# A decoder layer for four sequences on one core: PSUM banks in a ring, the causal mask on GpSimd, maxima as a stream, fill matmuls

## The chip, the cores and the metric

One core of a Trainium2 chip runs the kernel. The metric is device time in microseconds (us) of one execution, the median of several. Engines are named as in the profile: PE is TensorE (matmuls; PEld its weight loads), DVE is VectorE, ACT is ScalarE, POOL is GpSimd, SP issues DMAs. PSUM is the memory that PE writes its results to; it has eight banks of 512 fp32 columns.

## The reference

`x` is (4, 512, 512): four sequences of 512 tokens. For each, three residual blocks on layer-normalised input:

```python
x = x + attn(layernorm(x))      # 16 query heads of 32, one shared key and value head, causal
x = x + xattn(layernorm(x), fside, ctx)   # two SmoothQuant int8 linears with silu(gate) * up between
x = x + ffn(layernorm(x))       # gated, 1376 hidden, with shared LoRA and 8 rank-8 experts, top 2
```

The part that the change touches is the attention:

```python
scores = einsum('bqhd,bkd->bhqk', q, k) * scale
scores = where(tril, scores, finfo.min)
attn = softmax(scores, axis=-1)
ctx = einsum('bhqk,bkd->bqhd', attn, v)
```

## The kernel before

**Numbers.** Products that must keep fp32 accuracy are split in a high and a low part (fp32r) and made of three matmuls (`three`, L934 to L937). For the scores the three parts are stacked along the contraction: `qst` and `kst` have 96 rows, and two more rows carry the negated row maximum.

**Attention of one sequence (batch b).** Heads are worked on in four groups `g` of four. First the row maxima: `max` steps compute scores with queries on partitions (L1011), add the causal mask, DVE reduces each row (`negm`, L1295); a `rows` step transposes the 16 x 128 maxima (L1018) and SP moves them by DMA into `qst`. Then 16 steps (g, kt), kt from 3 down to 0: `scores` computes the scores again transposed, keys of tile kt on partitions and n = 512 - 128 kt queries along the columns (L1031); ACT takes the exponential into `probs` (L811); `values` multiplies them with v and with ones into `av` and `den` (L1045). `sums` and `context` normalise (DVE L1310, L1315, L1318), `split_context` makes the high (ACT) and low part (POOL L707), `out` is the output projection. The values of a step are placed behind the scores of the next, and `probs` holds two steps.

**Masks.** Both kinds of scores get their causal mask from PE: before the scores, matmuls of the identity with a mask tile in bf16 write -1e38 or 0 into PSUM with start=True (L1007 for the maxima, L1029 for the transposed scores), and the scores are added on them.

**PSUM.** `slots` are two places of two banks each, handed out in turn (`Tenants`) to every step of attention and of the middle block; `av` and `den` have a bank each; `ring` is two single banks for weight preparation and feed-forward. Whoever claims a place waits until the tenant before it has been read. A `max` unit has 2 or 4 heads spread over both banks of its slot (6 units for each group of heads, `MAX_GROUPS`), a `scores` step is two pairs of heads, one head in each bank.

**Order.** Steps come from four streams: A (attention), L (middle block: a serial chain with DVE, ACT and POOL), F (feed-forward, nearly all matmuls) and W (weights split once and stored). Hand-made strings of letters (`FIRST`, `SECOND`, `STEADY`, `LAST`) say which stream gives the next step; every engine runs its part of all steps in this one order. The `max` steps are part of A, at places that `MAX_AMONG` and `MAX_BEFORE` set. Attention of b = 0 runs with W beside it, then attention of b = 1 with the middle block of b = 0, and from the first `gate` step on F runs beside both.

## Time and profile before

| | us |
|---|---|
| median of 3 runs (1016.59 to 1024.69) | 1017.0 |
| the profiled execution | 1015.68 |
| its span, first to last instruction | 1013.9 |
| PE busy | 923.5 |
| DVE busy | 616.7 |
| ACT busy | 313.1 |
| POOL busy | 248.5 |

Busy is the union of an engine's instructions. A matmul's time in the trace includes its way through the array, so consecutive matmuls overlap in it: what one costs PE is read from start to start. The granted clock is 1.00 at 2.4 GHz and one half at 1.2 GHz; a mean over a stretch lies between. "<-" in a row of waits names what the engine waited for.

### The profile page before, as it was taken

What the parts mean: (1) busy time and instruction counts of PE and PEld (TensorE: products, weight loads), DVE (VectorE), ACT (ScalarE), POOL (GpSimd) and SP (SyncE); (2) the same over time, 40 slices, a digit from 0 to 9 for tenths busy, and PEclk for the clock granted to TensorE, in tenths of its full rate; (3) what the DMA queues carried; (4) which work ended last, traced back from release to release, by engine and by line L of the source; (5) the groups of instructions that cost most, each with busy time, mean ns of one, the idle gap of its engine ahead of it and who ended that gap; (6) DMA issues with size and microseconds to landing.
All of it is one profiled execution on the core that took longest, in us unless ns stands there. A gap on an engine that the chain in (4) does not pass through costs nothing.

```text
span 1013.9 us, 13146 instructions
## 1 busy us (share of the span) xinstructions
PE 923.5 (91%) x5206; PEld 654.6 (65%) x5214; DVE 616.7 (61%) x865; ACT 313.1 (31%) x496; POOL 248.5 (25%) x217
## 2 busy tenths in 40 slices
PE   2898899587999999999999999999979999779997
PEld 1664456454457776667577776666757787568785
DVE  2345768778687687767565886765477565332222
ACT  2323442244353215342423135333222431121110
POOL 3612322421543022123210131231204033011110
PEclk9857979688799999999999999999999999999999
DMA  8963651832666843348344733354335455525442
GB/s 277 312 189 116 233 216 24 246 128 88 238 197 253 202 172 123 126 171 340 116 154 93 230 123 104 147 226 141 107 140 199 152 185 209 205 94 206 161 170 89
DMA packets 42913, 174.98 MB, mean 173 GB/s; under 512 B 5404, under 2 KB 8220, under 8 KB 32868
## 3 DMA queue, kind: packets, MB, share of 16 engines
q1 hardware_dynamic: 36804, 119.09, 34.7%
q10 hardware_dynamic: 6048, 55.05, 14.9%
q8 instruction: 42, 0.69, 0.3%
q14 instruction: 19, 0.16, 0.0%
HBM read 127.52 MB, written 33.75 MB: 159 GB/s over the span
## 4 chain that ended last, share of the span: by engine, by line
PE 74%; DVE 13%; issue 4%; DMA 3%; SPq 3%; ACT 2%; POOL 1%; POOLq 0%; DVEq 0%; ACTq 0%
PE ring L935 12%; PE ring L937 11%; PE ring L936 11%; PE av L1045 4%; PE slot L1031 4%; DVE negm L1295 4%; PE ring L1177 3%; PE den L1045 3%; PE slot L1011 3%; SPq L573 3%; PE slot L935 3%; PE slot L936 2%; PE slot L937 2%; PE slot L1114 2%; PE slot L1029 2%
## 5 line engine op out<-in xcount | busy, mean ns | idle before, releaser
L734 POOL TENSOR_TENSOR hd_l<-hd,hd_h 128x512 fp32r<-128x512 f32 x44 | 57.7, 1312 | 401.2 <-ACT hd_h L909 401.2
L935 PE MATMUL ring<-xT_h,gu 128*128 128x512 f32 x352 | 145.6, 414 | 5.0 <-DVE gated L1502 2.9
L936 PE MATMUL ring<-xT_l,gu 128*128 128x512 f32 x352 | 138.4, 393 | 0.0
L937 PE MATMUL ring<-xT_h,gu 128*128 128x512 f32 x352 | 138.3, 393 | 0.0
L1295 DVE TENSOR_REDUCE negm<-slot 128x4 f32<-128x512 f32 (+2 forms) x96 | 98.6, 1043 | 59.6 <-PE slot L1011 59.0
L811 ACT ACTIVATE probs<-slot 128x256 f32<-128x256 f32 (+3 forms) x128 | 85.0, 700 | 89.8 <-PE slot L1031 89.8
L935 PEld LDWEIGHTS ring<-xT_h,gu 128*128 128x128 f32 x352 | 66.8, 190 | 29.4 <-issue 11.5
L937 PEld LDWEIGHTS ring<-xT_h,gu 128*128 128x128 f32 x352 | 66.6, 189 | 14.9
L1541 DVE TENSOR_TENSOR total<-ring,total 128x512 f32<-128x512 f32 x64 | 44.0, 688 | 51.0 <-PE ring L937 50.9
L1031 PE MATMUL slot<-qst,kst 98*128 98x128 f32 (+3 forms) x256 | 74.8, 387 | 0.0
L936 PEld LDWEIGHTS ring<-xT_l,gu 128*128 128x128 f32 x352 | 67.0, 190 | 11.6
L1011 PE MATMUL slot<-kst,qst 96*128 96x128 f32 (+3 forms) x256 | 73.4, 397 | 0.0
L935 PE MATMUL ring<-dn,hd_h 128*128 128x512 f32 x176 | 70.1, 398 | 0.2 <-DVE ad_sum L1521 0.2
L937 PE MATMUL ring<-dn,hd_l 128*128 128x512 f32 x176 | 69.2, 393 | 0.0
L936 PE MATMUL ring<-dn,hd_h 128*128 128x512 f32 x176 | 69.1, 393 | 0.0
L909 ACT ACTIVATE hd_h<-hd 128x512 fp32r<-128x512 f32 x44 | 27.8, 631 | 119.1 <-DVE hd L1513 119.1
L905 ACT ACTIVATE gated<-ring 128x512 f32<-128x512 f32 x44 | 26.3, 599 | 122.5 <-PE ring L1177 122.3
L1513 DVE SCALAR_TENSOR_TENSOR hd<-gated,ring 128x512 f32<-128x512 f32 x44 | 30.2, 687 | 51.7 <-PE ring L1177 36.1
L1502 DVE SCALAR_TENSOR_TENSOR gated<-gated,ring 128x512 f32<-128x512 f32 x44 | 29.9, 680 | 50.5 <-ACT gated L905 50.5
L1315 DVE RECIPROCAL rden<-rden 128x256 f32<-128x256 f32 x32 | 55.8, 1744 | 0.1
L1029 PE MATMUL slot<-mask_bf 128*128 128x128 bf16 x256 | 38.8, 236 | 16.9 <-DVE negm L1295 7.7
L1045 PE MATMUL av<-probs,v 128*32 128x512 f32 (+3 forms) x512 | 52.3, 484 | 1.3 <-DVE cx L1310 1.1
(194 smaller groups left out, 1754.2 us busy)
## 6 DMA issues: line engine op xcount, KB each, us to landing
gu<-gu_parts ACTq DMA_DIRECT2D x42, 1280.0 KB, 5.5
dn<-dn_parts SPq DMA_DIRECT2D x12, 1728.0 KB, 7.7
gu_parts<-gu SPq DMA_DIRECT2D x11, 1280.0 KB, 5.7
qst<-qT_h SPq DMA_DIRECT2D x64, 128.0 KB, 2.4
raw_gu<-gu SPq DMA_DIRECT2D x11, 640.0 KB, 7.3
dn_parts<-dn SPq DMA_DIRECT2D x11, 576.0 KB, 7.7
dn<-dn_parts SPq DMA_DIRECT2D x4, 1152.0 KB, 5.1
x_in<-x SPq DMA_DIRECT2D x8, 512.0 KB, 4.8
```

Source lines behind the costliest of these rows:

```text
L734: pool.tensor_tensor(hd_l[:, i, :], hd[:, i, :], hd_h[:, i, :].bitcast(F32), ALU.subtract).then_inc(hd_lo.sem, 1)
L811: act.activation(probs[:, 2 * (step % 2) + pr, :, 0:n], slots[SLOT["scores", b, step, pr]][:, :, 0:n], ACT.Exp, scale=SCALE).then_inc(p_re ...
L935: pe.matmul(out_, w_hi_, m_hi_, start=start, stop=False, skip_group_check=True)
L936: pe.matmul(out_, w_hi_, m_lo_, start=False, stop=False, skip_group_check=True)
L937: return pe.matmul(out_, w_lo_, m_hi_, start=False, stop=stop, skip_group_check=True)
L1011: mm = pe.matmul(ps[:, bank, at * n:(at + 1) * n], qst[0:KROWS, 4 * g + h0 + h, qt * P:(qt + 1) * P], kst[0:KROWS, 0:n], start=False, stop ...
L1029: pe.matmul(ps[:, j, 0:P], mask_bf[:, 0, :], mask_bf[:, 2, :], start=True, stop=False, skip_group_check=True)
L1031: mm = pe.matmul(ps[:, j, 0:n], kst[0:KROWS + 2, kt * P:(kt + 1) * P], qst[0:KROWS + 2, 4 * g + 2 * pr + j, kt * P:T], start=False, stop=T ...
L1045: mm = pe.matmul(to[HD * c:HD * c + HD, kt * P:T], weights, probs[:, 2 * (step % 2) + c // 2, c % 2, 0:n], start=(kt == TT - 1), stop=(kt ...
L1295: dve.tensor_reduce(negm[:, h0:h0 + heads, qt].rearrange("p (a c) -> p a c", a=2), slots[SLOT["max", b, g, i]][:, :, 0:heads // 2 * n].rea ...
L1315: dve.reciprocal(rden[:, cols], rden[:, cols]).then_inc(rden_ready.sem, 1)
L1541: dve.tensor_tensor(total[:, tt, :], ring[RING["down", b, s, tt]][:, :], total[:, tt, :], ALU.add)\
```

## The change

Five edits in one.

1. **Banks.** The four banks of the two slots become one ring of single banks. `Banks.claim` hands out one, or two neighbouring ones for the tenants in `BANK_WIDTH`; two at the end of the ring start again at bank 0. It waits for the release of each bank taken. A `q` step takes a bank of its own where two shared a slot.
2. **Units of one bank.** `MAX_GROUPS` is 11 units for each group of heads (4 heads of 128 columns; 2 of 256, twice; 1 of 384 and 1 of 512, four times each), `SCORES` splits each step in the same way: 1, 2, 4 and 4 units for kt = 3, 2, 1, 0. So there are 176 units of each kind for 96 `max` units and 128 pairs.
3. **The transposed scores' mask** is no longer added by PE (L1029 goes, 256 matmuls). ACT's exponential signals `p_exp`, and POOL then sets the upper part of the diagonal 128 x 128 block of each head in `probs` to 0 with an affine select; `values` wait for POOL. The bank is free as soon as ACT has read it.
4. **Maxima** are a stream X of their own, and one string `TURNS` gives the whole order, anew.
5. **Fills.** A digit n in `TURNS` is n matmuls of the bf16 identity with 256 columns of `mask_bf` into the ring bank that is next in turn, after its last reader and without claiming it. There are 428 of them in 154 places; 94 stand before the first transposes, 226 between the first `max` unit and the first `gate` step, 89 behind that. PE waits for the masks at its start.

```diff
+class Banks:
+    def claim(self, eng, key, signal, value):
+        first, width = bank_after(self.next, BANK_WIDTH.get(key[0], 1))
+        assert self.table[key] == (first, width), key
+        for bank in range(first, first + width):
+            if bank in self.left and (bank == first or self.left[bank] != self.left[first]):
+                eng.wait_ge(*self.left[bank])
+        for bank in range(first, first + width):
+            self.left[bank] = (signal.sem, value)
+        self.next = first + width
+        return self.banks[:, first:first + width, :]
...
-MAX_GROUPS = ((0, 0, 4), (1, 0, 4), (2, 0, 2), (2, 2, 2), (3, 0, 2), (3, 2, 2))
+    def upcoming(self, eng):
+
+        place = self.n % 2
+        if place in self.left:
+            eng.wait_ge(*self.left[place])
+        return self.places[place]
...
+BANKS = 4
+BANK_WIDTH = {"turn1": 2, "out": 2, "turn": 2, "s_rows_ps": 2, "turn_a": 2, "turn_w": 2, "product0": 2, "product1": 2}
+MAX_GROUPS = [(qt, h, min(4, TT // (qt + 1))) for qt in range(TT) for h in range(0, 4, min(4, TT // (qt + 1)))]
...
+SCORES = [[(h, min(4, TT // (TT - kt))) for h in range(0, 4, min(4, TT // (TT - kt)))] for g, kt in STEPS]
...
+def bank_after(bank, width):
+    return (0 if bank + width > BANKS else bank), width
+
+
+def maxima_steps(b):
+
+    for g in range(4):
+        for i in range(MG):
+            yield ("max", b, g, i)
...
-    "AAAAAAAAAAAAAAWAWWAAWAAAWAAAAAWWAAAAAAAAAAAAAAAAAAAAAAAAAAAWAWWAAAAAWAAWAAAAAAWAAAAWAAAAAAAAAAAAAAAAAAAAAAAAAA"
...
+TURNS = (
+    "A1A111114111111111114111111414111AA4444111111111111194111141AA1114A14AAAAA1AAA1W41WWAAWAX14XX11X1114X1XXX41XXW"
...
+            def scores(b, step, unit):
+                h0, heads = SCORES[step][unit]
+                at = 4 * (step % 2) + h0
+                pool.wait_ge(p_exp.sem, p_exp.at(b, SCORES_TO[step] + unit + 1))
+                pool.affine_select(probs[:, at:at + heads, 0:P], probs[:, at:at + heads, 0:P], [[0, heads], [1, P]], ALU.is_ge, 0.0,
+                                   base=0, channel_multiplier=-1).then_inc(p_ready.sem, 1)
...
+            pe.wait_ge(masks_ready.sem, 2)
+
+            def fill(n):
+
+                ps = in_ring.upcoming(pe)
+                for _ in range(n):
+                    pe.matmul(ps[:, 0:2 * P], mask_bf[:, 0, :], mask_bf[:, :, :], start=True, stop=True, skip_group_check=True)
...
-                for pr in range(2):
-                    ps = in_slots.claim(pe, ("scores", b, step, pr), p_ready, p_ready.at(b, 2 * step + pr + 1))
-                    for j in range(2):
-                        pe.matmul(ps[:, j, 0:P], mask_bf[:, 0, :], mask_bf[:, 2, :], start=True, stop=False, skip_group_check=True)
-                    for j in range(2):
-                        mm = pe.matmul(ps[:, j, 0:n], kst[0:KROWS + 2, kt * P:(kt + 1) * P],
-                                       qst[0:KROWS + 2, 4 * g + 2 * pr + j, kt * P:T], start=False, stop=True, skip_group_check=True)
-                    mm.then_inc(t_ps.sem, 1)
+                done = SCORES_TO[step] + unit + 1
+                ps = in_slots.claim(pe, ("scores", b, step, unit), p_exp, p_exp.at(b, done))
+                for h in range(heads):
+                    mm = pe.matmul(ps[:, 0, h * n:(h + 1) * n], kst[0:KROWS + 2, kt * P:(kt + 1) * P],
+                                   qst[0:KROWS + 2, 4 * g + h0 + h, kt * P:T], start=True, stop=True, skip_group_check=True)
+                mm.then_inc(t_ps.sem, 1)
...
-                pe.wait_ge(p_ready.sem, p_ready.at(b, 2 * step + 2))
+                pe.wait_ge(p_ready.sem, p_ready.at(b, SCORES_TO[step + 1]))
```

PE in attention of batch 0, before, from the second group's maxima to the first values (L1007 and L1029 are masks, L1011 maxima, L1031 transposed scores, L1045 values):

```order
L1007 MATMUL slot<-mask_bf 128x128 x2
L1011 MATMUL slot<-kst,qst 128x384 x2
L1029 MATMUL slot<-mask_bf 128x128 x2
L1031 MATMUL slot<-qst,kst 128x128 x2
L1029 MATMUL slot<-mask_bf 128x128 x2
L1031 MATMUL slot<-qst,kst 128x128 x2
L1007 MATMUL slot<-mask_bf 128x128 x2
L1011 MATMUL slot<-kst,qst 128x384 x2
L1007 MATMUL slot<-mask_bf 128x128 x2
L1011 MATMUL slot<-kst,qst 128x512 x2
```

The same place now (L1053 is the maxima's mask, L1056 maxima, L1074 transposed scores, L981 fills, L1088 values):

```order
L1074 MATMUL slots<-qst,kst 128x128 x4
L1053 MATMUL slots<-mask_bf 128x512
L1056 MATMUL slots<-kst,qst 128x128 x4
L981 MATMUL ring<-mask_bf 128x256
L1074 MATMUL slots<-qst,kst 128x256 x2
L981 MATMUL ring<-mask_bf 128x256
L1053 MATMUL slots<-mask_bf 128x2x128
L1056 MATMUL slots<-kst,qst 128x256 x2
L981 MATMUL ring<-mask_bf 128x256
L1074 MATMUL slots<-qst,kst 128x256 x2
```

Masks ahead of the transposed scores are gone, the maxima are those of the third group (two groups ahead of the scores, where they were one ahead), and every unit is followed by one of the other kind.

POOL, now, in attention of batch 2 with the middle block and feed-forward beside it (L743 is the selection, L776 the low part of a hidden tile, L764 the scaling of the middle block's weights, L755 its square root):

```order
L743 AFFINE_SELECT probs<-probs 128x4x128
L743 AFFINE_SELECT probs<-probs 128x2x128
L776 TENSOR_TENSOR hd_l<-hd,hd_h 128x512
L743 AFFINE_SELECT probs<-probs 128x2x128
L755 TENSOR_TENSOR sc<-sc,half 128x4
L743 AFFINE_SELECT probs<-probs 128x128
L776 TENSOR_TENSOR hd_l<-hd,hd_h 128x512
L743 AFFINE_SELECT probs<-probs 128x128 x3
L764 TENSOR_TENSOR w_raw_137<-w_raw_137,rows 128x512 x4
L743 AFFINE_SELECT probs<-probs 128x128 x4
```

Before, POOL had no part between the exponential and the values; there the selections now stand in line with the work of the other streams.

## Rows read from the trace of the kernel before

**Rows 1.** The page: span, busy time of engines, granted clock in 40 slices
```profile
span 1013.9 us, 13146 instructions
PE 923.5 (91%) x5206; PEld 654.6 (65%) x5214; DVE 616.7 (61%) x865; ACT 313.1 (31%) x496; POOL 248.5 (25%) x217
...
PEclk9857979688799999999999999999999999999999
```

**Rows 2.** Busy time by stage: stretch, its length, engines (instructions), clock, DMA share, GB/s
```profile
0.00:46.00 46.00, 22.50 (x101) 17.14 (x102) 12.45 (x22) 15.54 (x24) 21.85 (x27) 0.98 0.87 284
46.00:150.00 104.00, 93.31 (x604) 53.80 (x604) 62.05 (x74) 35.72 (x57) 27.29 (x24) 0.75 0.58 202
150.00:322.00 172.00, 145.93 (x923) 93.04 (x923) 132.90 (x178) 68.55 (x104) 61.21 (x51) 0.85 0.52 173
322.00:750.00 428.00, 419.71 (x2495) 299.87 (x2498) 291.19 (x415) 139.85 (x229) 91.84 (x80) 1.00 0.47 161
750.00:900.00 150.00, 135.17 (x635) 105.21 (x638) 88.46 (x135) 39.91 (x62) 32.16 (x25) 0.98 0.45 165
900.00:1013.90 113.90, 106.88 (x457) 85.49 (x455) 29.66 (x43) 13.56 (x22) 14.17 (x11) 0.98 0.43 155
```

**Rows 3.** Waits from 46 to 322 us: total, times, longest
```profile
DVE negm L1295 <- PE slot L1011: 39.6, 24, 4.5
ACT probs L811 <- PE slot L1031: 38.1, 30, 4.0
...
PE slot L1029 <- DVE negm L1295: 7.7, 15, 1.1
```

**Rows 4.** Timeline of PE at full clock: start, duration, instruction
```profile
429.02 0.39 PE L936 MATMUL ring<-dn,hd_h 128*128 128x512 f32 x1
429.25 0.39 PE L937 MATMUL ring<-dn,hd_l 128*128 128x512 f32 x1
429.48 0.29 PE L1029 MATMUL slot<-mask_bf 128*128 128x128 bf16 x2
429.58 0.60 PE L1031 MATMUL slot<-qst,kst 98*128 98x384 f32 x2
430.01 0.29 PE L1029 MATMUL slot<-mask_bf 128*128 128x128 bf16 x2
```

**Rows 5.** Waits of PE: the first transposes
```profile
PE slot L961 <- DVE x_in L1256: 18.6, 1, 18.6
```

**Rows 6.** Groups of DVE: shapes, count, busy us, mean ns, idle before
```profile
L1295 DVE TENSOR_REDUCE negm<-slot 128x2 f32<-128x1024 f32 x32 | 38.4, 1220 | 3.9 <-PE slot L1011 3.6
L1295 DVE TENSOR_REDUCE negm<-slot 128x4 f32<-128x512 f32 x16 | 11.0, 685 | 18.7 <-PE slot L1011 18.6
```

**Rows 7.** Timeline of PE at the low clock
```profile
51.89 0.39 PE L1007 MATMUL slot<-mask_bf 128*128 128x128 bf16 x2
...
53.05 0.44 PE L1007 MATMUL slot<-mask_bf 128*128 128x128 bf16 x2
```

**Rows 8.** Groups of POOL by shape
```profile
L734 POOL TENSOR_TENSOR hd_l<-hd,hd_h 128x512 fp32r<-128x512 f32 x44 | 57.7, 1312 | 401.2 <-ACT hd_h L909 401.2
...
L707 POOL TENSOR_TENSOR hT_l<-cx,hT_h 128x256 fp32r<-128x256 f32 x32 | 25.3, 789 | 92.2 <-ACT hT_h L823 92.2
...
L674 POOL TENSOR_TENSOR dn<-raw_dn,dn 128x64 fp32r<-128x64 f32 x11 | 3.9, 357 | 0.0
```

**Rows 9.** Timeline of POOL and DVE at 94 us
```profile
94.15 2.89 POOL L667 TENSOR_TENSOR gu<-raw_gu,gu 128x1280 fp32r<-128x1280 f32 x1 [2.36 <-ACT gu L767]
94.46 2.86 DVE L1318 TENSOR_TENSOR cx<-cx,rden 128x256 f32<-128x256 f32 x1
```

**Rows 10.** The context product of DVE: durations min/median/max, and its group
```profile
L1318 DVE TENSOR_TENSOR cx<-cx,rden x32: 424/426/2857, 94.5 to 724.1; 128x256 f32<-128x256 f32 x32
```
```profile
L1318 DVE TENSOR_TENSOR cx<-cx,rden 128x256 f32<-128x256 f32 x32 | 22.4, 701 | 1.1
```

More of the change, by code:

```diff
@@ L90 @@
 STEPS = [(g, kt) for g in range(4) for kt in reversed(range(TT))]
+SCORES = [[(h, min(4, TT // (TT - kt))) for h in range(0, 4, min(4, TT // (TT - kt)))] for g, kt in STEPS]
+SCORES_TO = [sum(len(units) for units in SCORES[0:step]) for step in range(len(STEPS) + 1)]
 MLP_STEPS = ("turn", "colmax", "ratio", "s_cols", "s_rows_ps", "s_rows", "scale", "rowmax_a", "rowmax_w",
@@ L126, in attention_steps @@
             yield ("rows", b, g + 1)
-        yield ("scores", b, step)
+        for unit in range(len(SCORES[step])):
+            yield ("scores", b, step, unit)
         if step == 7:
@@ L272, in in_order @@
-    assert len(order) == sum(len(steps) for steps in streams.values())
+    order = [("fill", int(name)) if name.isdigit() else next(left[name]) for name in TURNS]
+    assert len([step for step in order if step[0] != "fill"]) == sum(len(steps) for steps in streams.values())
     return order
@@ L279, in tenants_of @@
 def tenants_of():
-    slots, ring = [], []
+    slots, ring, bank = {}, [], 0
     for step in ORDER:
         name = step[0]
-        if name in ("turn1", "kv", "v", "max", "rows", "out", "w_turn") or name in MLP_TENANTS:
-            slots.append(step)
-        elif name == "q" and step[2] % 2 == 0:
-            slots.append(step)
-        elif name == "scores":
-            slots += [(*step, pr) for pr in range(2)]
+        if name in ("turn1", "kv", "q", "v", "max", "rows", "scores", "out", "w_turn") or name in MLP_TENANTS:
+            slots[step] = bank_after(bank, BANK_WIDTH.get(name, 1))
+            bank = sum(slots[step])
         elif name == "prep_gu":
@@ L295, in tenants_of @@
             ring.append(step[:-1])
-    return {key: n % 2 for n, key in enumerate(slots)}, {key: n % 2 for n, key in enumerate(ring)}
+    return slots, {key: n % 2 for n, key in enumerate(ring)}
 SLOT, RING = tenants_of()
@@ L407, in program @@
             ("d_raw", [P, TT, INNER], (xT_at + 8192, wqkv_at + 8192)), ("wrow", [P, D], (a_at, wqkv_at + 16384))))
[L409 removed]
+        slots = ctx.enter_context(nc.psum_tensor("slots", [P, BANKS, T], F32))
         av = ctx.enter_context(nc.psum_tensor("av", [P, T], F32))
@@ L474, in gu_tile, with slot @@
             return n % 2, n // 2 + 1, n % FT
+        def slot(*key):
+            first, width = SLOT[key]
+            return slots[:, first:first + width, :]
         def hid_slot(b, f):
@@ L831, in s_rows_ @@
                 act.wait_ge(s_rows_ps.sem, s_rows_ps.at(b, n + 1))
-                act.activation(rows[:, :, 0:width], slots[SLOT["s_rows_ps", b, n]][:, :, 0:width], ACT.Copy).then_inc(s_rows.sem, 1)
+                act.activation(rows[:, :, 0:width], slot("s_rows_ps", b, n)[:, :, 0:width], ACT.Copy).then_inc(s_rows.sem, 1)
             def half_of(n, h):
```

162 lines of the change are left out of this document (75 added, 87 removed).

## The prediction

> **What bounds the kernel now.** I read the page first [rows 1]: TensorE (PE) is busy 91% of the 1013.9 us span, VectorE (DVE) 61%, GpSimd (POOL) 25%. The strip of granted clock shows something beside that: full speed nearly throughout the second half, but 5 to 8 tenths in many early slices. So the stages have different limits, and I cut the span at what the kernel does, with one row per stage [rows 2]. From 322 us on, where feed-forward matmuls of the previous batch fill every gap, PE is busy 661.8 of 691.9 us at a clock of 0.98 to 1.00: that stage is PE's. From 46 to 322 us (attention of batch 0, then attention of batch 1 beside the MLP of batch 0) PE shows 239.2 of 276 us busy, but at a clock of 0.75 and 0.85. A granted mean of 0.75 between levels of 1 and one half means that half of those 104 us were at 1.2 GHz; of the 172 us at 0.85, three tenths. Together some 104 us at the low level. The waits of that stretch say who waits [rows 3]: DVE's row maxima wait 39.6 us for PE's scores in 24 places, ACT's exponentials 38.1 us, and PE's scores wait for DVE to hand back a slot. Each has one unit in hand and the other idles: two slots are a lock-step. DVE works 62.05 + 132.90 = 195 us of the 276 there, 71%, and no engine is full. That is the stretch in which a ring of banks can give time; after 322 us only a change in PE's work can.
>
> The profiled execution took 1015.68 us, 1.3 below the median of 1017.0. Terms are summed against 1015.7, and 1.3 is added at the end.
>
> **1. The masks that leave PE.** Before, a pair of transposed-score matmuls is preceded by two bf16 mask matmuls. Starts of consecutive lines [rows 4]: a 512-column matmul begins 0.23 us after the one before it; the pair of masks and two 384-column scores runs from 429.48 to 430.01, 0.53 us. Without masks two of 384 columns are 2 x 0.23 x 384/512 = 0.34 us. So a pair costs 0.19 us for its masks: their 0.10, and 0.09 because the first f32 weights behind bf16 work load in the open. There are 128 such pairs, 64 of them in batches 2 and 3, behind 322 us where PE is full: 64 x 0.19 = -12 us. The other 64 (12 us, double at the low clock) lie in the stretch that no engine fills; they are part of term 4.
>
> **2. Maxima in smaller units.** The mask columns stay. But a unit is now one bank: 11 units a group of heads for 6, so 11 returns from bf16 to f32 for 6: 5 x 0.09 = 0.45 us, 8 groups behind 322 us: 3.6, less the second mask's fixed part. I take +3. Between 0 and +6.
>
> **3. Fills.** 428 matmuls of 256 columns, in 154 places. At half a 512-column spacing each is 0.115 us [rows 4]. 339 stand ahead of the first feed-forward matmul, 89 behind it, in 22 runs: 89 x 0.115 = 10.2, and 22 x 0.09 = 2.0 for the returns to f32. Where PE would stand idle anyway they cost nothing; PE's idle time behind 322 us is 30.1 us [rows 2]. I take half, +6; ends 0 and +12. A fill also waits for the ring bank that the next claim would take, so it can only advance a wait that was due. The first 94 stand before the first transposes, where PE sits idle 18.6 us for the first normalisation [rows 5]. They start when the masks are converted; 94 x 0.115 = 11 us, more at the low clock, and so they may overrun by 0 to 3 us and give that back in the first projections, which then begin warm: 0, between -3 and +3.
>
> **4. The stretch from 46 to 322 us.** DVE's work there is the floor. Reductions [rows 6]: 685 ns for 512 elements, 1220 for 1024, so 1.045 ns an element and 150 ns an instruction; 384 elements are 551 and 768 are 953. A group was 0.69 + 3 x 1.22 + 2 x 0.95 = 6.3 us, and is 3 x 0.69 + 4 x 0.55 + 4 x 0.69 = 7.0. Eight groups fall in the stretch: +6, so DVE has 201 us. What four banks change is how well this is packed: PE can run units ahead of DVE, one wide unit no longer holds both banks of a slot, and maxima can be threaded between single score units (order, second pair of pieces). PE gets 226 x 0.115 = 26 us of fills there and has room for them, and the clock should stand higher: the two stages of low clock are those in which PE stands idle most (10.7 of 104 and 26.1 of 172 us), and at the low level a pair of masks and two 512-column maxima takes 1.16 us from start to start [rows 7] instead of 0.10 + 0.09 + 2 x 0.23 = 0.65, which DVE waits out. At the present packing (71%) the stretch would be 285 us, +9; at 95%, which nothing here suggests is reachable with the moves of q through DMA and the layer's serial chain inside it, 212 us, -64. I choose 87%, nearer to the upper end because masks, clock and bank waits all go at once: 231 us for 276, **-45 us**. The first feed-forward matmul should then start near 277 us.
>
> **5. Idle time behind 322 us.** PE's 30.1 us: 14.8 of them from 750 to 900 us, where the MLP of batch 3 has only one stream beside it. The new order mixes finer; I take a fifth, -6; ends 0 and -20.
>
> **6. GpSimd's selections.** 176 new instructions, one for each unit, of 512, 256 or 128 elements. The trace has no such instruction. Nearest rows [rows 8]: 357 ns for 64 elements with two inputs, 789 for 256, 1312 for 512. By a line between them 128 elements are 0.50, and a group is 1.31 + 2 x 0.79 + 8 x 0.50 = 6.9 us, 110 us in all; with each at 0.36 it is 63, with each at 1.31, 231. GpSimd is busy 249 of 1014 us, so the work fits. Hidden is it where the next step's score matmuls run between a selection and the values that need it, which the order does everywhere; what it adds is a link in the chain exp, selection, values. Queued behind GpSimd's instruction are the splits of context and hidden tiles, for which ACT or PE's low parts wait. I set the link at 0.
>
> What is not free is DVE. A 256-element product with both inputs in SBUF takes 424 ns at least, and 2.86 us when it began beside a 2.89 us GpSimd instruction; over 32 its mean is 701 [rows 9], [rows 10], so 32 x 0.275 = 8.8 us lost beside 249 us of GpSimd work. With 110 us more, 44% on top: +4 on this line, and some as much on the others of two SBUF inputs. I take **+5**, between 0 and +12. The Trainium skill, "SBUF — State Buffer", section "Who interferes with whom", says that the two engines share a port pair as an exclusive lock, taken by the first to issue, and that a reduction never takes it. The trace agrees on the product. By that rule the maxima, most of DVE's new work, lose nothing, and a selection that comes second waits for DVE's whole instruction too; the first alone would leave the term at 5, the second alone would bring the contention rival's 984. The rival's chance itself rests on the 2.86 us of [rows 9].
>
> **Sum.** -12 + 3 + 6 + 0 - 45 - 6 + 5 = -49: 1015.7 - 49 = 966.7, and 968 against the median. With the packing between 82% and 91% (-31 and -55) and the small terms half-way to one side (6 either way) this case's own range is 952 to 988.
>
> **Rivals.**
> *Lock-step stays.* The dependencies, not the slots, set the packing from 46 to 322 us: the same engines wait for the same results. For it: ACT's waits for PE are as large as DVE's, and a bank count does not shorten exp to values. Against: PE's waits name reduced slots. Then the stretch gives only its masks less the added reductions, -6, and the rest -12 + 3 + 6 + 5 = +2: 1013. Chance 0.12.
> *GpSimd ends last (slower).* Values, "PE av", wait for a selection that is queued behind a hidden-tile split (1.31 us) or a 2.9 us weight split, themselves waiting for ACT: GpSimd stands 401 us before that split already, waiting for ACT [rows 8]. Each of 64 steps loses x; from x = 49/64 = 0.77 us it eats the gain. With a split and a selection ahead of it in two steps of three, 64 x 1.9 x 2/3 = 81: 968 + 81 = 1049; with half of that covered by the neighbour step, still 1009. Against: other streams' matmuls stand between. For slower, 1045. Chance 0.07.
> *Port contention and fills cost all their bounds.* +12 + 12 + 6 instead of +14: 984; where contention also takes a fifth of term 4, 993. Chance 0.08.
> *Everything packs.* 95% in the stretch (-64), idle behind it -20, fills hidden: -64 - 20 - 12 + 3 + 0 + 2 = -91: 926. Chance 0.18. For it: the maxima's and exponentials' waits of the stretch, 77.7 us together [rows 3], are all of the kind that banks can take away, and the order fits maxima, a DVE load, between score units, an ACT load.
>
> **How the numbers follow.** The forecast case has the remaining 0.55: 968. A measurement here can tell about 1%. Faster by over 1% (below 1007) holds forecast, packing and contention, 0.81, and the nearer part of the lock-step case and its neighbourhood, 0.05: 0.86. Within 1%: 0.07. Slower: 0.07. The range leaves out half of the packing case and the slower one: 930 to 1014.
>
> **What would show it.** Right: the first gate matmul (gu into ring) near 277 instead of 322 us; granted clock of 0.95 or more from 46 us to there; "DVE negm waits for PE slot" below 15 us in that stretch; PE idle behind it about 25 us and the distance from the first gate matmul to the end near 685 us, where it was 691.9. Selections near 0.5 us at 128 elements; the cx product's mean above 750 ns. Wrong: "PE av waits for POOL probs" among the largest waits (the slower rival); the first gate matmul at 315 us or later (lock-step); the clock again at 0.8, with fills in place, would say that fills do not hold it and takes about a third of term 4.

## The result and the profile after

The changed kernel takes 1003.07 us (median, 999.05 to 1007.04), the kernel before beside it 1020.3 us: ratio 0.984, 95% interval 0.981 to 0.988. It is faster by 1.6%, 16 us. The forecast was 5%, 49 us. It lies inside the whole range of 930 to 1014 us, but outside the forecast case's own 952 to 988. The profiled execution took 999.05 us, span 997.3, 4 us under its kernel's median. That of before (1015.68) lies 1.3 us under the 1017.0 of its first three runs and 4.6 under this 1020.3, and its mean granted clock over the whole execution was 0.943, where 43 later executions of that kernel had 0.924 to 0.941. So what the traces say of the clock before is on the high side.

The page of the changed kernel answers to [rows 1]:

```profile
span 997.3 us, 13830 instructions
PE 938.5 (94%) x5362; PEld 672.2 (67%) x5370; DVE 614.4 (62%) x945; ACT 315.5 (32%) x544; POOL 310.1 (31%) x393
...
PEclk9887999698799999999999999999999999999999
```

PE is 15 us busier in a span 17 us shorter. The clock is higher in the first part, but digits of 6 to 8 are still there. The same cut by stage as in [rows 2], with an additional cut at 326 us:

```profile
46.00:150.00 104.00, 103.39 (x747) 65.72 (x746) 66.48 (x101) 38.79 (x71) 44.69 (x69) 0.90 0.66 232
150.00:294.50 144.50, 125.81 (x793) 77.37 (x793) 114.26 (x173) 62.69 (x108) 71.81 (x89) 0.82 0.55 182
294.50:326.00 31.50, 31.45 (x152) 25.33 (x148) 22.33 (x38) 10.55 (x16) 2.81 (x4) 1.00 0.24 76
326.00:750.00 424.00, 412.14 (x2372) 293.23 (x2375) 292.42 (x448) 138.47 (x247) 122.29 (x169) 1.00 0.48 164
750.00:900.00 150.00, 141.33 (x697) 110.64 (x699) 78.92 (x127) 38.58 (x60) 33.58 (x26) 1.00 0.48 173
```

From 46 to 150 us PE is busy 103.39 of 104 us. The idle time that the ring of banks was to remove is gone, and the clock is 0.90, not 1.

**Which marker to compare.** The first gate matmul moved from 322.6 to 294.5 us. That overstates the gain: the new order has gate steps ahead of more of the attention of batch 1. The first gated product on DVE stands behind about the same work in both orders: up to it, DVE works 205.7 us in each of the two kernels without fills that differ only in the order (from the experiments below). Its instructions between 300 and 360 us, before and then after (columns: count, durations min/median/max in ns, first to last start in us):

```profile
L1502 DVE SCALAR_TENSOR_TENSOR gated<-gated,ring x2: 677/678/679, 339.8 to 350.9; 128x512 f32<-128x512 f32 x2
```
```profile
L1544 DVE SCALAR_TENSOR_TENSOR gated<-gated,ring x4: 672/676/679, 326.0 to 359.9; 128x512 f32<-128x512 f32 x4
```

339.8 became 326.0, 13.8 us earlier. From there to the end it was 1013.9 - 339.8 = 674.1 us and is 997.3 - 326.0 = 671.3. "Ahead" and "behind" below mean these two parts.

The waits of the changed kernel from 46 to 326 us answer to [rows 3]:

```profile
POOL probs L743 <- ACT probs L853: 37.3, 29, 6.5
...
ACT probs L853 <- PE slots L1074: 28.9, 24, 6.0
...
DVE negm L1338 <- PE slots L1056: 25.8, 24, 3.4
```

DVE's wait for PE fell from 39.6 to 25.8 us, in 24 places again. The row that says what replaced the old limit is the share of lines in the chain of work that ended last, from 46 to 330 us, before and after:

```profile
by line: DVE negm L1295 11.4%; PE av L1045 7.3%; PE slot L1011 6.3%; PE slot L1031 6.1%; PE den L1045 6.0%; DVE rden L1315 4.2%; PE ring L951 4.1%; PE ring L945 3.9%; PE slot L935 3.7%; PE slot L937 3.5%; issue 3.5%; PE slot L936 3.5%; PE s
```
```profile
by line: PE ring L981 9.8%; PE slots L1056 8.4%; PE av L1088 6.8%; PE slots L1074 6.4%; PE den L1088 5.4%; PE slots L984 5.2%; PE slots L986 5.1%; PE slots L985 5.1%; PE ring L1000 4.0%; PE ring L994 3.9%; PE slots L1053 3.3%; issue 3.3%; S
```

DVE's reductions led it with 11.4%. They are no longer among its first twelve; the fills (L981) lead with 9.8%, and then come matmuls only. The lock-step was dissolved, and PE's own time, at the clock it was granted, took its place.

### The profile page after: what moved, and what is told of

Read it like the earlier page. It is cut to its first block, busy times and chain, and to the rows that moved or that the text cites. A ratio compares the mean times of both kernels' runs of the same rounds, so it can differ in the third digit from the quotient of the medians.

```text
span 997.3 us, 13830 instructions
## 1 busy us (share of the span) xinstructions
PE 938.5 (94%) x5362; PEld 672.2 (67%) x5370; DVE 614.4 (62%) x945; ACT 315.5 (32%) x544; POOL 310.1 (31%) x393
## 4 chain that ended last, share of the span: by engine, by line
PE 81%; DVE 6%; issue 3%; ACT 3%; DMA 3%; SPq 2%; POOL 1%; POOLq 0%; DVEq 0%
PE ring L984 12%; PE ring L985 12%; PE ring L986 12%; PE ring L981 5%; PE slots L1056 4%; PE av L1088 4%; PE slots L1074 4%; PE ring L1220 4%; PE den L1088 3%; PE slots L984 3%; PE slots L986 3%; PE slots L985 3%; SPq L608 2%; PE slots L1157 2%; PE slots L1053 2%
## 5 line engine op out<-in xcount | busy, mean ns | idle before, releaser
L776 POOL TENSOR_TENSOR hd_l<-hd,hd_h 128x512 fp32r<-128x512 f32 x44 | 57.3, 1302 | 287.7 <-ACT hd_h L951 287.7
L984 PE MATMUL ring<-xT_h,gu 128*128 128x512 f32 x352 | 143.2, 407 | 0.4 <-DVE gated L1544 0.3
L1338 DVE TENSOR_REDUCE negm<-slots 128x1 f32<-128x384 f32 (+3 forms) x176 | 107.2, 636 | 58.2 <-PE slots L1056 57.2
L986 PE MATMUL ring<-xT_h,gu 128*128 128x512 f32 x352 | 137.5, 391 | 0.0
L853 ACT ACTIVATE probs<-slots 128x512 f32<-128x512 f32 (+1 forms) x176 | 90.7, 556 | 97.4 <-PE slots L1074 97.0
L743 POOL TENSOR_SCALAR_AFFINE_SELECT probs<-probs 128x128 f32<-128x128 f32 (+2 forms) x176 | 67.3, 394 | 125.6 <-ACT probs L853 124.8
L1056 PE MATMUL slots<-kst,qst 96*128 96x128 f32 (+3 forms) x256 | 87.2, 416 | 0.0
L1074 PE MATMUL slots<-qst,kst 98*128 98x128 f32 (+3 forms) x256 | 68.5, 357 | 13.2 <-DMA qst<-negm_hl 12.1
L981 PE MATMUL ring<-mask_bf 128*128 128x256 bf16 x428 | 67.0, 300 | 7.8 <-ACT mask_bf L789 7.8
L1074 PEld LDWEIGHTS slots<-qst,kst 98*128 98x128 f32 x256 | 44.6, 202 | 34.2 <-DMA qst<-negm_hl 13.2
L981 PEld LDWEIGHTS ring<-mask_bf 128*128 128x128 bf16 x428 | 42.0, 107 | 31.1 <-issue 15.1
L1053 PE MATMUL slots<-mask_bf 128*128 128x128 bf16 (+2 forms) x176 | 47.5, 270 | 12.5 <-issue 6.9
```

The source lines that it names most:

```text
L743: pool.affine_select(probs[:, at:at + heads, 0:P], probs[:, at:at + heads, 0:P], [[0, heads], [1, P]], ALU.is_ge, 0.0, base=0, channel_mul ...
L776: pool.tensor_tensor(hd_l[:, i, :], hd[:, i, :], hd_h[:, i, :].bitcast(F32), ALU.subtract).then_inc(hd_lo.sem, 1)
L853: act.activation(probs[:, at:at + heads, 0:n], slot("scores", b, step, unit)[:, 0, 0:heads * n].rearrange("p (h n) -> p h n", n=n), ACT.Ex ...
L981: pe.matmul(ps[:, 0:2 * P], mask_bf[:, 0, :], mask_bf[:, :, :], start=True, stop=True, skip_group_check=True)
L984: pe.matmul(out_, w_hi_, m_hi_, start=start, stop=False, skip_group_check=True)
L986: return pe.matmul(out_, w_lo_, m_hi_, start=False, stop=stop, skip_group_check=True)
```

## The experiments

Ratios are to the kernel before, run beside each on the same chip (medians 1018.6, 1019.6 and 1020.5 us in the three sets).

| kernel | us | ratio, 95% | first gated product | from it to the end |
|---|---|---|---|---|
| before | 1020.3 | 1 | 339.8 | 674.1 |
| selection alone | 1009.8 | 0.992 (0.989 to 0.995) | 346.8 | 662.7 |
| + banks, units, old order | 1015.6 | 0.996 (0.993 to 0.999) | 340.9 | 673.1 |
| + new order | 1007.4 | 0.990 (0.987 to 0.992) | 334.2 | 671.3 |
| + fills: the changed kernel | 1003.1 | 0.984 (0.981 to 0.988) | 326.0 | 671.3 |

The last two columns are from one profiled execution each. Executions of one kernel spread over 3 to 16 us. Two pairs of kernels below are the same up to the gated product and have it at 326.0 and 325.8, and at 313.4 and 317.7 us. So differences of up to 4 us in a column decide nothing.

### The parts, one after the other

**The selection alone**, in the kernel before:

```diff
+            def scores(b, step):
+                for pr in range(2):
+                    at = 2 * (step % 2) + pr
+                    pool.wait_ge(p_exp.sem, p_exp.at(b, 2 * step + pr + 1))
+                    pool.affine_select(probs[:, at, :, 0:P], probs[:, at, :, 0:P], [[0, 2], [1, P]], ALU.is_ge, 0.0, base=0, channel_multiplier=-1)...
-                    for j in range(2):
-                        pe.matmul(ps[:, j, 0:P], mask_bf[:, 0, :], mask_bf[:, 2, :], start=True, stop=False, ...)
```

> The kernel before with the transposed scores' mask on GpSimd alone: order, slots and pairs as before, no fills. By the prediction's term 1 (64 pairs x 0.19 us behind 322 us, and the rest in the stretch where nothing is full): 1003 to 1009 us. Theory G (a selection is a new link between exp and values and costs what the masks gave): 1014 to 1024 us. Fully converted masks in both stages (128 pairs, some at the low clock): 990 to 996 us.

Measured: 1009.76, ratio 0.992. Behind, 674.1 became 662.7: -11.4, term 1's -12. Ahead, 339.8 became 346.8: +7.0, although PE has 64 pairs of masks less to do. The granted clock fell there (columns as in [rows 2]; before, the same rows read 0.74 and 0.82):

```profile
46.00:140.00 94.00, 83.68 (x452) 46.25 (x452) 52.88 (x65) 28.57 (x47) 32.27 (x47) 0.64 0.53 181
140.00:294.50 154.50, 130.33 (x738) 79.51 (x740) 111.62 (x142) 61.19 (x90) 64.72 (x72) 0.77 0.48 157
```

**No mask on the transposed scores at all**: as above, but GpSimd does nothing and values wait for ACT. The causal mask of the transposed scores is left out.

> The kernel before without any mask on the transposed scores: neither PE's matmuls nor GpSimd's selection; values wait for the exponential alone. Against the kernel with the selection alone (1009.8 us, its first gated instruction of DVE at 346.8 us where before has 339.8). Theory L (the selection is a link that costs some 7 to 13 us in the stretch ahead of 340 us, where it queues behind weight splits): 996 to 1002 us, first gated instruction at 334 to 340 us. If the link is free and the stretch got longer by the lower clock: 1007 to 1012 us, first gated instruction at 345 us or later.

Measured: 1004.31 (1002.93 to 1005.95), ratio 0.985 (0.982 to 0.988), between the two ranges expected. First gated product at 338.8, 662.3 from there to the end. Against the selection alone: 8.0 us earlier ahead, the same behind (662.3, 662.7). So the selection costs 7 to 8 us ahead, in the old order, and behind neither link nor contention costs anything that shows. That the cost ahead is the link exponential, selection, values is argued and not shown: in that stretch the weight loads of the values into `av` wait 3.2 us for selections, and without them 2.0 us for exponentials, and PE is idle 35.7 and 34.6 us. The 64 pairs of masks ahead moved the gated product by 1 us (339.8 to 338.8) and not by 12. The clock fell here too, to 0.68 from 46 to 140 us where it was 0.74; more of it below.

**Banks, units and selection in the order of before**, no fills: the old strings; each old `max` or `scores` step gives its one-bank units in its old place.

```diff
+def units_of(step):
+    if step[0] == "max":
+        _, b, g, i = step
+        qt, h0, heads = OLD_GROUPS[i]
+        return [("max", b, g, n) for n, (q, h, _) in enumerate(MAX_GROUPS) if q == qt and h0 <= h < h0 + heads]
```

> The changed kernel's ring of four banks, its one-bank units and GpSimd selections, but steps in the order of before (each old max or scores step replaced by its units) and no fills. Theory B (banks are what helps, as term 4 had it): 975 to 990 us, first gate matmul at 300 us or earlier. Theory D (chains and their order set the stretch): within 4 us of the kernel before with the selection alone, first gate matmul at 310 to 322 us. If smaller units cost more than banks give: slower than that by 5 us or more.

Measured: 1015.58, ratio 0.996. Against the selection alone: 5.9 us won ahead, 10.4 lost behind, where term 2 said +3.

**The new order without fills:**

```diff
-    order = [("fill", int(name)) if name.isdigit() else next(left[name]) for name in TURNS]
+    order = [next(left[name]) for name in TURNS if not name.isdigit()]
```

> The changed kernel without its 428 fills; all else the same. Theory F (fills take PE time on the path: the chain of the changed kernel gives them 5% of its span): faster than the changed kernel, 975 to 993 us, ratio to before 0.955 to 0.975. Theory C (fills stand where PE waits and hold the clock, as the prediction had it): slower, 1008 to 1020 us, the mean clock down from 0.962 to 0.94 or less, and the first gate matmul at 305 us or later instead of 294.5. Theory D (the stretch from 46 to 322 us is set by the chains of results, fills are neutral): 1000 to 1006 us.

Measured: 1007.43 (1005.27 to 1021.77), ratio 0.990; first gate matmul at 302.7, the profiled execution's mean clock 0.924. That is close to theory C, whose range began at 1008. The order won 6.7 us ahead and 1.8 behind; the fills win 8.2 more ahead and nothing behind. The stretch by stage (columns as in [rows 2]), before, without fills, and changed:

```profile
46.00:140.00 94.00, 83.31 (x543) 47.96 (x546) 56.77 (x68) 33.61 (x54) 26.55 (x23) 0.74 0.55 192
140.00:294.50 154.50, 128.43 (x829) 79.80 (x825) 113.89 (x146) 60.78 (x93) 48.01 (x39) 0.82 0.48 157
```
```profile
46.00:140.00 94.00, 90.89 (x516) 49.80 (x519) 58.44 (x90) 36.42 (x67) 40.39 (x67) 0.67 0.68 243
140.00:294.50 154.50, 135.90 (x743) 85.71 (x738) 120.03 (x180) 61.36 (x104) 67.69 (x81) 0.76 0.49 164
```
```profile
46.00:140.00 94.00, 93.39 (x689) 57.17 (x688) 60.62 (x93) 37.34 (x69) 43.95 (x68) 0.89 0.69 243
140.00:294.50 154.50, 135.81 (x850) 85.93 (x851) 120.12 (x181) 64.14 (x110) 72.55 (x90) 0.83 0.54 178
```

PE is busier (83.31 to 90.89 of 94 us), yet the granted clock is lower (0.74 to 0.67) and DVE got through only 58.44 us of work instead of 56.77. With fills the clock is 0.89, and part of PE's time goes to the fills.

**What the clock took.** This is the main reading of the study. The same view from 46 us to each kernel's first gated product, for before, the selection alone, before without the masks of the maxima (tried further down), the new order without fills, the changed kernel, and the changed kernel without the masks of the maxima:

```profile
46.00:339.80 293.80, 256.99 (x1607) 161.06 (x1609) 204.81 (x274) 111.46 (x171) 88.51 (x75) 0.82 0.53 178
46.00:346.80 300.80, 265.07 (x1482) 162.51 (x1485) 205.26 (x274) 111.54 (x171) 115.52 (x139) 0.77 0.52 173
46.00:339.50 293.50, 260.66 (x1510) 161.13 (x1509) 202.83 (x274) 112.19 (x171) 88.63 (x75) 0.78 0.53 177
46.00:334.20 288.20, 266.44 (x1465) 164.49 (x1467) 205.66 (x312) 112.36 (x195) 117.98 (x163) 0.76 0.54 185
46.00:326.00 280.00, 260.64 (x1685) 168.43 (x1685) 203.06 (x311) 112.03 (x195) 119.31 (x162) 0.87 0.56 189
46.00:313.40 267.40, 247.04 (x1600) 160.08 (x1599) 201.87 (x312) 112.15 (x195) 119.63 (x162) 0.88 0.58 198
```

From such rows: PE's idle time; what the low clock took, one minus the clock times the length; and the rest, which is an estimate of PE's work at full clock (the clock has two digits, so the last two columns are good to 1 or 2 us). Beside them is the mean clock of whole executions, over all runs of a kernel.

| from 46 us to the first gated product | length | PE idle | low clock | the rest | clock, all runs |
|---|---|---|---|---|---|
| before | 293.8 | 37 | 53 | 204 | 0.933 |
| selection alone | 300.8 | 36 | 69 | 196 | 0.925 |
| no mask on the transposed scores | 292.8 | 35 | 61 | 197 | 0.926 |
| before, maxima without masks | 293.5 | 33 | 65 | 196 | 0.925 |
| + banks, units, old order | 294.9 | 33 | 65 | 197 | 0.927 |
| + new order | 288.2 | 22 | 69 | 197 | 0.921 |
| + fills: the changed kernel | 280.0 | 19 | 36 | 224 | 0.957 |
| fills doubled | 288.1 | 16 | 23 | 249 | 0.970 |
| changed, maxima without masks | 267.4 | 20 | 32 | 215 | 0.958 |

So the clock fell when mask matmuls left PE, with the old slots and the old order, and not because banks or order packed PE better: each of the three ways of taking masks out of the kernel before gives 7 to 8 us of PE work and takes 9 to 16 us more by the low clock. The traces overstate the fall, as the one of before had a high clock; over all runs it is 0.933 to 0.925, some 8 us of an execution. The masks are bf16 matmuls as the fills are, and in the kernel before they held the clock up as fills do. The new order then cut PE's idle time by 11 us, at a slightly lower clock still (0.921). The fills add 27 us of work and take away 33 of low clock. Fills in the kernel before, with its masks and its order, were not tried, so the record does not say how much of the gain they would give alone.

### What a fill costs and what it brings

**Fills only ahead of the first gate step** (89 fewer):

```diff
+    first = next(n for n, step in enumerate(order) if step[0] == "gate")
+    order = order[:first] + [step for step in order[first:] if step[0] != "fill"]
```

> The changed kernel with only the 339 fills that stand ahead of the first gate matmul; the 89 behind it go. Theory F: 990 to 995 us (9 to 12 us of PE time come back). Theory C or D: within 3 us of the changed kernel, 1000 to 1006 us.

Measured: 1001.4 (996.61 to 1009.81), ratio 0.985 (0.980 to 0.991), the same as the changed kernel. The fills behind neither cost nor bring time that shows, though over all runs the clock is 0.951 without them and 0.957 with them.

**The 226 fills between the first `max` and the first `gate` step doubled:**

```diff
+    order = [("fill", 2 * step[1]) if step[0] == "fill" and a < n < z else step for n, step in enumerate(order)]
```

> The changed kernel with twice the 226 fills between the first maximum and the first gate matmul. Theory P (PE is the path of this stretch, now that DVE's maxima no longer are: a fill costs 0.11 us there and what it gives back is clock only as long as the clock is low; 10% to 17% of the stretch is low): clock of the stretch 0.93 or more, 226 x 0.11 = 25 us more less at most 15 us of clock: 1010 to 1020 us. Theory C (the clock is what limits the stretch): faster, 990 to 1000 us. Theory D (chains of other engines set it, fills are hidden): 1000 to 1006 us.

Measured: 1011.52 (1007.76 to 1016.36), ratio 0.991 (0.988 to 0.994), slower than the changed kernel by 0.7% (7 us; the intervals just meet); first gated product at 334.1.

```profile
46.00:140.00 94.00, 94.00 (x799) 64.05 (x801) 56.48 (x89) 35.23 (x66) 39.97 (x66) 0.99 0.66 233
140.00:294.50 154.50, 138.33 (x903) 90.79 (x896) 118.92 (x181) 62.28 (x105) 69.10 (x81) 0.86 0.50 164
```

The first row has the clock I had forecast (0.99), and DVE did less there (56.48 us, where it did 60.62). Up to the gated product the second 226 fills take 13 us of low clock away and add 25 us of work. None (334.2), as placed (326.0), doubled (334.1): of the three, the number in the kernel is the best.

### Is DVE the limit ahead?

**Reductions over the diagonal 128 columns alone.** The shift of the softmax then comes from fewer keys; PE does what it did.

```diff
-slot("max", b, g, i)[:, 0, 0:heads * n].rearrange("p (h n) -> p h n", n=n),
+slot("max", b, g, i)[:, 0, 0:heads * n].rearrange("p (h n) -> p h n", n=n)[:, :, n - P:n],
```

> The changed kernel with DVE reducing only the diagonal tile of each head (128 columns) in the 176 maxima: some 3.2 us a group less, 51 us of DVE in all, 26 us of them ahead of the first gate matmul. The maximum over fewer keys is left as the shift. Theory P (PE is the path of the stretch, DVE is not): 996 to 1003 us, first gated instruction of DVE at 320 us or later (326.0 in the changed kernel). Prediction's term 4 (DVE's 201 us are the floor of the stretch): 15 to 25 us less, 978 to 988 us, first gated instruction at 300 to 311 us.

Measured: 1000.13 (993.6 to 1003.1), ratio 0.979 (0.975 to 0.984); first gated product at 319.9. DVE's busy time fell by 614.4 - 568.4 = 46 us in all; the time fell by 0.5%, 5 us, which the intervals do not separate from none. Up to the gated product DVE worked 180.5 us instead of 203.1, and 22.6 us less work brought it 6.1 us earlier. DVE is not the floor. In the kernel before this was not tried.

**The changed kernel without the masks of the maxima.** The shift then comes from more keys than the causal ones, which leaves the softmax as it is; DVE does what it did, PE 176 bf16 matmuls and 176 returns to f32 less.

```diff
-                pe.matmul(diagonal, mask_bf[:, 0, :], mask_bf[:, 1:2, :].to_broadcast([P, heads, P]), start=True, stop=False, ...)
...
-                                   kst[0:KROWS, 0:n], start=False, stop=True, skip_group_check=True)
+                                   kst[0:KROWS, 0:n], start=True, stop=True, skip_group_check=True)
```

> The changed kernel without the masks of the maxima: the 176 bf16 matmuls ahead of the maxima go, and the row maximum is taken over the whole diagonal tile, which is as good a shift for the softmax. Theory U (what the one-bank units cost is their returns from bf16 to f32, 0.14 us a unit with the mask): 88 units behind the first gate matmul x 0.14 = 12 us less, and 6 to 12 us less ahead of it: 980 to 987 us, ratio 0.962 to 0.969. Theory W (the units cost by waits for DVE, masks are hidden): 996 to 1004 us.

Measured: **982.3** (978.75 to 990.67), ratio 0.964 (0.959 to 0.969): 2.0% under the changed kernel, the fastest of all. First gated product at 313.4 (12.6 us earlier), 666.7 from there to the end (4.6 less). A unit of one 512-column maximum, in the changed kernel (a mask ahead of it) and without:

```profile
431.99 0.23 PE L1053 MATMUL slots<-mask_bf 128*128 128x128 bf16 x1
432.03 0.48 PE L1056 MATMUL slots<-kst,qst 96*128 96x512 f32 x1
432.35 0.39 PE L984 MATMUL ring<-xT_h,gu 128*128 128x512 f32 x1
```
```profile
416.35 0.40 PE L1053 MATMUL slots<-kst,qst 96*128 96x512 f32 x1
416.58 0.40 PE L984 MATMUL ring<-xT_h,gu 128*128 128x512 f32 x1
```

From start to start 0.36 us against 0.23: 0.13 us a unit, of which the mask's columns are 0.04 and the dearer return to f32 0.09.

**The same edit in the kernel before:**

> The kernel before without the masks of the maxima alone (the shift of the softmax then comes from more keys, which does not change the softmax; the transposed scores keep their mask). Theory U2 (a mask of the maxima costs PE its columns and the first f32 weights behind it, whatever the bank scheme): 192 bf16 matmuls and 96 returns go; behind the first gate matmul 48 units x 0.19 = -9 us, before it, where DVE waits for PE's unit, up to 48 x 0.4 = -19: 990 to 1008. Theory B (the saving of 20 us that the same edit gave in the changed kernel came from its one-bank units and the ring): within 1% of before, 1012 to 1020.

Measured: 1014.06 (1008.42 to 1017.1), ratio 0.993 (0.990 to 0.996), in theory B's range: 7 us, a third of what it gave in the changed kernel. First gated product at 339.5, where it was 339.8. The chain from 46 to 330 us still begins with DVE:

```profile
by line: DVE negm L1291 11.2%; PE av L1041 8.0%; PE slot L1027 7.7%; PE slot L1007 6.7%; PE den L1041 6.5%; PE ring L945 6.0%; PE ring L951 4.0%; PE slot L1025 3.9%; PE slot L935 3.7%; PE slot L937 3.6%; PE slot L936 3.5%; issue 2.7%; PE sl
```

One edit, ahead of the gated product: 0.3 us in the kernel before, 12.6 in the changed kernel. It is tempting to say that PE's work counts there only since the change. The table above says something else: the edit took 8 us of work off PE in the one and 9 in the other, and PE's idle time did not grow in either by more than 1 us (37 to 33, 19 to 20). What differs is the clock: 12 us more lost in the kernel before (0.74 to 0.65 from 46 to 140 us), 4 us less in the changed kernel. Over all runs it fell from 0.933 to 0.925 in the one and stayed (0.957, 0.958) in the other. Whether the lock-step would have hidden the saving at a held clock was not tried.

### The selection in the new kernel, and versions beyond

**The mask back on PE**, one bf16 matmul a unit, no selection:

```diff
+                pe.matmul(diagonal, mask_bf[:, 0, :], mask_bf[:, 2:3, :].to_broadcast([P, heads, P]), start=True, stop=False, ...)
...
-                pe.wait_ge(p_ready.sem, p_ready.at(b, SCORES_TO[step + 1]))
+                pe.wait_ge(p_exp.sem, p_exp.at(b, SCORES_TO[step + 1]))
```

> The changed kernel with the transposed scores' mask back on PE (one bf16 matmul in each of 176 units) and no selection on GpSimd. Theory U (in the new kernel PE's own work and its clock set the end nearly everywhere, so a mask costs what it takes on PE): 176 masks with the return to f32 behind each, about 0.19 us at full clock for 88 of them behind the first gate matmul, +12 to +17 us there, and about as much before it less the freed link exponential to values, +0 to +12; in all 1015 to 1028. Theory L (the selection stands on the chain exponential, selection, values, and what it saves is given back): 998 to 1006, with a first gated product at 320 us or earlier (326.0 in the changed kernel).

Measured: 1010.61 (1008.55 to 1016.87), ratio 0.991 (0.987 to 0.995). The selection is worth 0.7%, 7 us (the intervals just meet), below the range of the first theory (12 to 25) and above that of the second. In the trace, whose execution took 1016.87 us, the slowest of its six, the masks cost 15.4 us behind (686.7) and 2.4 ahead (328.4). Ahead they are 9 us of PE work, of which the clock gives 5 back (31 us lost to it, where the changed kernel loses 36); over all runs it is 0.967 against 0.957. The second theory wanted the gated product at 320 us or earlier, so the link does not explain this.

**Without masks of the maxima, and fills only ahead of the gate step; and with no fills at all:**

> The changed kernel without the masks of the maxima and without the 89 fills behind the first gate matmul. If those fills cost nothing (as taking them out alone moved 1003.1 to 1001.4): 978 to 983. If they keep the clock where masks no longer do: 985 to 992. If they are pure PE time there: 89 x 0.13 = -11, 970 to 975.

> The changed kernel without the masks of the maxima and without any fill. Fills are worth +4 to +8 us where the masks stand; where PE has less bf16 work of its own the clock should stand lower still. If fills are worth the same here: 984 to 992, with a granted clock near 0.67 from 46 to 140 us. If PE's freed time makes them needless: 976 to 982.

Measured: 987.18 (981.69 to 991.04), ratio 0.967 (0.963 to 0.970), and 995.81 (992.42 to 1003.44), ratio 0.978 (0.973 to 0.983). The first lies in the range of the second alternative (fills behind keep the clock: 0.950 over all runs without them, 0.958 with them), but 0.967 is not told apart from 0.964 with all fills. The second lies outside both of its ranges. It puts the fills ahead at 1.1%, 11 us (0.978 against 0.967), where they were 6 (0.990 against 0.984); the intervals do not show that they are worth more there. Its clock is 0.73 from 46 to 140 us, not the 0.67 that I had expected.

## Why the prediction was right and wrong

**Right: the direction, and the sum behind.** Terms 1, 2, 3, 5 and 6 gave -12 + 3 + 6 - 6 + 5 = -4 there; the gated marker gives 671.3 - 674.1 = -2.8. That is partly luck, as the terms one by one show:

| term | forecast | measured |
|---|---|---|
| 1, masks leave PE, behind | -12 | -11.4 alone |
| 2, maxima in one-bank units | +3 (0 to +6) | +10.4, all of banks and units, behind |
| 3, fills behind | +6 (0 to +12) | 0 |
| 4, the stretch ahead | -45 | -14 |
| 5, idle time behind | -6 | -2, from the order, within the spread |
| 6, contention with GpSimd | +5 | 0 |
| 6, the link exp, selection, values | 0 | the selection: +8 ahead, in the old order, by what path is open |

**The step that failed is term 4, at its first sentence:** "DVE's work there is the floor." I divided DVE's 201 us by a packing of 87%, got 231 us, and never asked whether PE fits into 231. Its row was there [rows 2]: PE was busy 93.31 + 145.93 = 239.2 us of the 276. Less the masks (12 us, "double at the low clock"), plus 26 of fills, that is 241 to 253 us. So the 231 needed a clock near 1 throughout, and that rested on one sentence, "the clock should stand higher". Among its reasons were the masks that go, and taking them away lowered the clock.

The table of the clock gives the account up to the gated product, by arithmetic and not by experiment. Before: PE idle 37 us, 53 lost to the low clock, 204 of work at full clock. After: 19, 36 and 224. So 17 us of idle time and 17 of low clock went, and 20 of work came: 27 of fills, less 8 of masks, and 1 with the units. The stretch is 13.8 us shorter, where term 4 had 45. I had said 0.95 for the clock; at that, 14 us would be lost to it and not 36, which is 22 of the 31 us that are missing. What kept the rest is in four slices of 20 us of the changed kernel:

```profile
140.00:160.00 20.00, 19.89 (x100) 15.43 (x100) 15.73 (x23) 5.78 (x8) 3.53 (x5) 1.00 0.33 108
160.00:180.00 20.00, 15.80 (x83) 12.42 (x81) 12.85 (x21) 3.07 (x4) 1.01 (x1) 0.83 0.72 160
180.00:200.00 20.00, 11.06 (x71) 8.87 (x72) 17.18 (x25) 7.65 (x13) 11.46 (x7) 0.66 0.29 100
...
260.00:280.00 20.00, 19.03 (x121) 10.36 (x119) 17.20 (x30) 10.21 (x20) 15.50 (x21) 0.72 0.85 293
```

From 160 to 200 us PE is idle 13 of 40 us, most of it in one wait. The scores of batch 1 need its first maxima, and DVE splits these (L1343) only when it has done the instructions of the middle block and of the weights that stand ahead in its order:

```profile
184.18 1.71 DVE L1441 TENSOR_TENSOR xn<-xn,rows 128x1024 f32<-128x1024 f32 x1
190.51 0.28 DVE L1343 TENSOR_TENSOR negm_hl<-slots,negm_hl 16x128 fp32r<-16x128 f32 x1
193.35 1.11 PE L1074 MATMUL slots<-qst,kst 98*128 98x128 f32 x4 [8.86 <-DMA qst<-negm_hl]
```

Four banks do nothing for that; another order there was not tried. At 260 us PE is busy 19 of 20 us at a clock of 0.72, fills included. My last line, "the clock again at 0.8, with fills in place, would say that fills do not hold it and takes about a third of term 4", was met (0.82 from 150 us to the first gate matmul), and two thirds of term 4 were missing, not one. The chain of waits, the reductions' trial (6.1 us ahead for 22.6 of DVE work), the masks taken out of the changed kernel (12.6 us ahead for 9 of PE work and 4 of low clock) and the doubled fills (8.1 us lost ahead) say that PE's own work, at the clock granted, sets the changed kernel's stretch, and DVE's does not.

**Term 2** went by five returns to f32 more in a group, at 0.09. Measured are 0.36 us for a unit of one 512-column maximum, 0.13 of that through its mask, and the whole step to banks and units costs 10.4 us behind. Which part is the returns and which is how the units fall among other streams in the old order was not tried apart; in the changed kernel taking all 88 masks out gave 4.6 us there, less than 88 x 0.13 = 11.

**Term 3.** Half of the fills' 12 us behind was guessed; with and without them the time was the same. The 94 fills at the start cost nothing, as forecast: the first reduction of a maximum begins at 45.0 us, before at 46.5.

**Term 6.** Selections took 336 ns at 128 elements where I had drawn a line to 500, and 67.3 us in all, not 110:

```profile
L743 POOL TENSOR_SCALAR_AFFINE_SELECT probs<-probs 128x128 f32<-128x128 f32 x128 | 41.3, 336 | 41.6 <-ACT probs L853 40.9
...
L743 POOL TENSOR_SCALAR_AFFINE_SELECT probs<-probs 128x256 f32<-128x256 f32 x32 | 15.2, 481 | 37.3 <-ACT probs L853 37.2
...
L743 POOL TENSOR_SCALAR_AFFINE_SELECT probs<-probs 128x512 f32<-128x512 f32 x16 | 10.8, 678 | 46.7 <-ACT probs L853 46.7
```

The line came from products with two inputs [rows 8]; a selection has one. The cx product was to rise above 750 ns and fell to 529, from 701 [rows 9, 10].

**The rivals.** *Lock-step stays* had the wrong mechanism, though its time (1013) lay nearer to 1003 than mine did: the lock-step went. *GpSimd ends last* happened at most in small, +8 us for the selection in the old order, on a path that was not shown, never near 0.77 us a step in the new one: the values' weight loads wait 6.8 us for a selection in the whole run, in 14 places. One place of it in the changed kernel, on POOL, DVE and PE:

```profile
219.68 1.35 DVE L1400 SCALAR_TENSOR_TENSOR th<-th,hid 128x1024 f32<-128x1024 f32 x1
219.89 3.56 POOL L743 TENSOR_SCALAR_AFFINE_SELECT probs<-probs 128x128 f32<-128x128 f32 x6
221.06 1.22 DVE L1401 SCALAR_TENSOR_TENSOR hid<-th,hid 128x1024 f32<-128x1024 f32 x1
...
222.49 0.16 PEld L1088 LDWEIGHTS av<-probs,v 128*32 128x32 f32 x8 [2.12 <-POOL probs L743]
```

Six selections take 3.56 us there, where six of 0.29 make 1.7. The first two take 1.29 us each; they overlap DVE's products of two SBUF inputs and last about as long as these; values wait 2.12 us. The Trainium skill, "SBUF — State Buffer", section "Who interferes with whom", gives the port pair to the engine that issues first; by that rule a selection that comes second waits for the whole instruction of DVE, and these rows agree. It is rare: 0.5 us apart behind the gated product between selecting and not selecting (662.7 and 662.3).

## What to carry to other kernels

When a wait between two engines is to go, work out what each engine of the pair would need in the new time, PE at the clock that its rows show, before you take the other one's work as the floor. Price a stretch at the low clock until a run shows the high one, and tune fills by count, as none and twice as many were both 8 us worse ahead. When you take matmuls away where PE stands at the low clock in part, read the clock again: the masks' time came back in part only, as the clock fell with them. And look for work that need not be done: the mask of the maxima only shifted a softmax, and leaving it out was worth 7 us before the change, when the clock fell with it, and 20 after it, when fills held the clock.

## What the runs showed of the hardware

- A PE that is busy nearly all the time can stand at the low clock: busy 90.89 of 94 us at 0.67 (no fills), 83.31 at 0.74 (before), 93.39 at 0.89 (with fills), 94.00 at 0.99 (doubled). A pair of masks with two 512-column maxima takes 1.16 us at the low clock [rows 7], where the prediction puts it together from rows at full clock as 0.65. So a busy share does not say how much work PE did.
- The clock went with the bf16 matmuls beside the f32 ones. Mean over all runs of a kernel: 0.933 before, 0.925 to 0.926 with either kind of mask gone; 0.921 without fills, 0.957 with them, 0.967 with the masks back as well, 0.970 with the fills doubled. The masks of the maxima leaving the changed kernel did not move it (0.958).
- At full clock a 512-column f32 matmul behind a bf16 mask costs 0.36 us with it, 0.23 alone; at 128 columns of mask, most of the 0.13 is the return and not the mask.
- GpSimd's affine select in place takes 0.34, 0.48 and 0.68 us for 128, 256 and 512 elements, and 1.29 us, twice, where one of 0.29 met a DVE product of two SBUF inputs of 1.35 and 1.22 us.
